# An unread 26-row product behind the second scores of the first attention, in the steps where the shared bank is free

## The reference

```
x = x + 0.5 * ffn0(layernorm(x))      # routed experts
x = x + attn0(layernorm(x))           # this case
x = x + 0.5 * ffn0(layernorm(x))
x = x + 0.5 * ffn1(...)
x = x + attn1(...)
x = x + 0.5 * ffn1(...)
```

```
qkv  = x @ qkv_w + qkv_b
attn = softmax(einsum('bnhd,bmhd->bhnm', q, k) * 8 ** -0.5)
out  = einsum('bhnm,bmhd->bnhd', attn, v) @ proj_w + proj_b
```

## Time and profile before

| what | us |
|---|---|
| median of 3 runs | 3365.65 |
| lowest, highest of them | 3340.04, 3366.84 |
| the profiled execution | 3353.67 |
| its span, first to last instruction | 3351.9 |
| first attention within the span | about 455 to 1335 |

### The profile page before, as it was taken

The page is one execution under the profiler, slowest core; times in us unless marked ns, Lnnn a source line. Parts: engine busy times, 40 slices in busy tenths (PEclk is TensorE's granted clock), DMA queues, the critical chain, the costliest instruction groups (busy, mean ns, idle before and its releaser), DMA issues. The chain is left out here.

```text
span 3351.9 us, 46625 instructions
## 1 busy us (share of the span) xinstructions
PE 2934.7 (88%) x15938; PEld 1757.2 (52%) x15938; DVE 2516.6 (75%) x6115; ACT 1773.0 (53%) x2711; POOL 928.1 (28%) x885
## 2 busy tenths in 40 slices
PE   6999959999999998899995689899799999989853
PEld 4666623443443443666663556566566666656432
DVE  6888767888888880788876797867366778797765
ACT  3444406777777775444435556454345555555544
POOL 2221121121111100212101355556323323343333
PEclk9999957999999996899995689989899999999965
DMA  4343432122122110343430000000000000000000
GB/s 127 77 100 80 95 102 93 57 93 84 66 93 84 66 49 6 111 93 79 101 77 1 1 7 20 19 19 19 32 13 13 13 7 14 13 7 26 7 7 25
DMA packets 71588, 167.20 MB, mean 50 GB/s; under 512 B 8792, under 2 KB 9400, under 8 KB 67128
## 3 DMA queue, kind: packets, MB, share of 16 engines
q1 hardware_dynamic: 69176, 160.03, 16.5%
q10 hardware_dynamic: 2176, 4.19, 0.3%
HBM read 120.67 MB, written 43.52 MB: 49 GB/s over the span
## 5 line engine op out<-in xcount | busy, mean ns | idle before, releaser
L706 DVE TENSOR_REDUCE att_mx<-att_pair 128x2 f32<-128x1024 f32 x512 | 617.0, 1220 | 132.5 <-PE att_pair L955 132.1
L881 ACT ACTIVATE att_pt<-att_pair 128x1024 f32<-128x1024 f32 x512 | 522.8, 1025 | 235.7 <-PE att_pair L965 233.1
L977 PE MATMUL att_o<-att_pt,att_vx 128*32 128x256 f32 x4096 | 335.5, 413 | 9.8 <-ACT att_oT L887 5.1
L955 PE MATMUL att_pair<-att_k,att_q 24*128 24x512 f32 x1024 | 272.4, 535 | 48.8 <-DMA att_k<-att_spread_k 14.2
L965 PE MATMUL att_pair<-att_q,att_k 26*128 26x512 f32 x1024 | 265.5, 520 | 0.0
L965 PEld LDWEIGHTS att_pair<-att_q,att_k 26*128 26x128 f32 x1024 | 98.5, 191 | 195.0 <-issue 168.1
L457 ACT ACTIVATE ffnA_h<-ffnA_up,b 128x512 f32<-128x512 f32 x144 | 98.7, 686 | 178.9 <-PE ffnA_up L105 177.2
L457 ACT ACTIVATE ffnB_h<-ffnB_up,b 128x512 f32<-128x512 f32 x144 | 98.6, 685 | 178.1 <-PE ffnB_up L105 176.4
L955 PEld LDWEIGHTS att_pair<-att_k,att_q 24*128 24x128 f32 x1024 | 100.3, 195 | 136.2 <-ACT att_pt L881 89.2
L977 PEld LDWEIGHTS att_o<-att_pt,att_vx 128*32 128x32 f32 x4096 | 91.6, 111 | 143.0 <-issue 123.4
L1897 ACT ACTIVATE att1k_sq<-att1k_k 128x512 f32<-128x512 f32 x128 | 76.2, 595 | 165.0 <-PE att1k_k L105 164.9
(11 more groups left out here) (538 smaller groups left out, 7787.8 us busy)
## 6 DMA issues: line engine op xcount, KB each, us to landing
ffnA_weights<-ffnA_weights SPq DMA_DIRECT2D x128, 256.0 KB, 5.6
att_q<-att_spread_q SPq DMA_DIRECT2D x16, 1024.0 KB, 4.9
att_k<-att_spread_k SPq DMA_DIRECT2D x16, 1024.0 KB, 4.8
att_spread_q<-att_qhi SPq DMA_DIRECT2D x32, 256.0 KB, 2.5
att_spread_k<-att_khi SPq DMA_DIRECT2D x32, 256.0 KB, 3.3
twk_hi<-ffnB_weights SPq DMA_DIRECT2D x32, 256.0 KB, 3.9
twk_lo<-ffnB_weights SPq DMA_DIRECT2D x32, 256.0 KB, 5.0
tgk_hi<-ffnB_weights SPq DMA_DIRECT2D x32, 256.0 KB, 6.0
```

Source lines behind the costliest of these rows:

```text
L706: v.tensor_reduce(top[b % 2][:, t, h:h + 2], pair("s", k)[:, :].rearrange("p (h n) -> p h n", h=2), AX, ALU.max, negate=True).then_inc(mx, 1)
L881: a.activation(pt[k % 8][:, :, :].rearrange("p h n -> p (h n)"), pair("t", k)[:, :], ACT.Exp, scale=scale).then_inc(p_, 1)
L955: last = pe.matmul(pair("s", k)[:, (j - j0) * 512:(j - j0 + 1) * 512], qb[b % 3][r, u, t * P:(t + 1) * P], kb[b % 3][r, u, :], start=True, ...
L977: last = pe.matmul(obank[j * BLOCK:(j + 1) * BLOCK, cols], vxb[b % 3][:, t, 4 * u + j, :], pt[(2 * g + j // 2) % 8][:, j % 2, cols], start ...
```

## The change

After the second scores of a step (`again`) TensorE now calls `keep_clock`. In steps in which no value in `misc` is still to be read it issues one more product of 26 rows by 512 columns, from the first head strip (partitions 0 to 25) of the same unit and tile, into `misc`. Nobody reads it, and it signals nothing. Before it stands `misc_free` of the next use of misc, so TensorE waits there for the reader of the last one. The step of each use is written beside it in `uses_of_misc`, and `misc_idle` holds the steps from two after a use up to the one before the next.

```diff
-        yield from (("x", 0), ("q", 0), ("k", 0), ("v", 0))
+        yield from ((-1, "x", 0), (-1, "q", 0), (-1, "k", 0), (-1, "v", 0))
...
-                yield "maxima", m - 1
+                yield STEPS * m + 2, "maxima", m - 1
...
-    misc_uses = list(uses_of_misc())
+    misc_order = list(uses_of_misc())
+    misc_uses = [(kind, k) for _, kind, k in misc_order]
     misc_number = {use: n for n, use in enumerate(misc_uses)}
+    misc_idle = {step: (kind, k) for (last, _, _), (next_, kind, k) in zip(misc_order, misc_order[1:]) for step in range(max(last, 0) + 2, next_)}
...
+        def keep_clock(k):
+
+            step = k + LAG
+            if step in misc_idle:
+                b, u, t, _ = place(k)
+                r = slice(0, SHIFTED)
+                misc_free(pe, *misc_idle[step])
+                pe.matmul(misc[:, :], kb[b % 3][r, u, t * P:(t + 1) * P], qb[b % 3][r, u, :], start=True, stop=True)
+
...
                 if 0 <= k < total:
                     again(k)
+                    keep_clock(k)
                 if STEPS * m + n + 1 < total:
                     scores(STEPS * m + n + 1)
```

More of the change, by code:

```diff
@@ L646, in uses_of_misc @@
             if now:
-                yield "maxima", m - 1
+                yield STEPS * m + 2, "maxima", m - 1
             if new:
-                yield "x", m + 1
+                yield STEPS * m + 5, "x", m + 1
             if old:
-                yield "out", UNITS * (m - 2) + 2
+                yield STEPS * m + 7, "out", UNITS * (m - 2) + 2
             if new:
-                yield "q", m + 1
-                yield "k", m + 1
+                yield STEPS * m + 9, "q", m + 1
+                yield STEPS * m + 13, "k", m + 1
             if old:
-                yield "out", UNITS * (m - 2) + 3
+                yield STEPS * m + 15, "out", UNITS * (m - 2) + 3
             if new:
-                yield "v", m + 1
+                yield STEPS * m + 17, "v", m + 1
             if old:
-                yield "final", m - 2
-                yield "proj", m - 2
+                yield STEPS * m + 21, "final", m - 2
+                yield STEPS * m + 23, "proj", m - 2
             if now:
-                yield "out", UNITS * (m - 1)
-                yield "out", UNITS * (m - 1) + 1
-    misc_uses = list(uses_of_misc())
+                yield STEPS * m + 25, "out", UNITS * (m - 1)
+                yield STEPS * m + 30, "out", UNITS * (m - 1) + 1
+    misc_order = list(uses_of_misc())
+    misc_uses = [(kind, k) for _, kind, k in misc_order]
     misc_number = {use: n for n, use in enumerate(misc_uses)}
+    misc_idle = {step: (kind, k) for (last, _, _), (next_, kind, k) in zip(misc_order, misc_order[1:]) for step in range(max(last, 0) + 2, next_)}
     def misc_free(pe, kind, k):
```

## The result

| | before | after |
|---|---|---|
| median of the runs, us | 3363.7 | 3416.1 |
| lowest, highest | 3340.0, 3366.8 | 3406.0, 3425.3 |
| ratio | | 1.0171, 95% interval 1.0115 to 1.0226 |
| the profiled execution, its span | 3353.7, 3351.9 | 3425.3, 3423.1 |
| mean granted clock | 0.908 | 0.893 |

The change costs 1.7%, by the ratio some 57 us (39 to 76); the two medians lie 52 us apart. Ratios compare fast runs alone: a run over 1.5% above the fastest of its kernel is left out. The forecast was 38 us, and the median lies inside its range. The span of the profiled execution is 71 us longer. The first attention alone became 79.6 us longer, and 8.5 of that came back in the keys stage of the second attention (615.1 to 606.6 us). That stage has none of the change, and over all 14 profiles it took between 606.6 and 619.3 us, at a mean clock between 0.81 and 0.83.

The account below looks back on a forecast made before the run. The prediction took a ring of second scores, exponential, first scores and weighing as the limit. 30.2 us for 13 full groups, 3 for m = 1 and 4.7 for the last groups made 38, on 3359.7: 3398 us, range 3372 to 3425.

Parts of the forecast that it names:

- The ring: First attention: second scores, exponential, first scores into that bank pair, weighing, next second scores; said to hold the pace.
- the three waits: Steps 11, 4 and 19 of each group: TensorE waits for misc's reader, costing 0.80, 0.48 and 0.71 us.
- the 0.10 of step 20: Step 20 of a full group: some 0.1 us of the added product's delay is left.
- step 4: Step 4 of a group: the product waits for the reader of the maxima, moving the weighing by 0.48 us.
- The seven other products: Steps 0, 1, 12, 20, 27, 28, 29: nothing except 0.10 us in step 20 and 0.23 in step 28.
- the walk: Step-by-step timing of the group from 703.09 in the first attention: the change adds 2.32 us per group.
- The clock: Granted clock in the first attention: no net change taken, nothing added to the forecast.
- The rival that the waits lower the clock: Clock falls at one of three thinner places in most groups; 13 groups add 30 us: 3428 us, chance 0.16.
- the balance: Products of steps 27 to 29 ahead of low-clock stretches set against places thinned by waits: clock effect nothing.
- the busy but slow stretch at the end: From 1258.8 to 1306.9, TensorE busy 44.8 of 48.1 us yet near the lower clock; added products should hardly raise it.
- The group m = 1: First attention, group m = 1: the same three waits and one more, mostly at the lower clock, 3 us.
- The late part: Last three groups of the first attention: 1.2 us in m = 15, 2.8 in m = 16, 0.7 in m = 17.

Follow-up runs that it names:

- The waits alone: The change with all its waits for the bank's reader but without the added product: 1.0088 of the kernel before, groups 51.50 us apart.
- the run with late steps: The change with its product only from the third step behind a use of misc on, five per full group: 1.0023 of the kernel before.
- the last run: The change with its wait in step 11 kept and only the product of step 11 left out: 1.0129 of the kernel before.
- the repeat: The change once more, unaltered, timed in another batch with a second profile: 1.0240 of the kernel before, median 3429.5 us.

## Why the prediction was right, and where its size was off

**The ring and the waits: right.** The largest term was the three waits, counted in full because no idle TensorE stands behind them. By the distances from the start of the first step named to the end of the last one:

| steps | before, us | after, us | more | forecast |
|---|---|---|---|---|
| 4 to 7 | 5.83 | 6.27 | 0.44 | 0.48 |
| 11 to 13 | 5.16 | 5.96 | 0.80 | 0.80 |
| 19 to 23 | 8.38 | 9.10 | 0.72 | 0.71 + 0.10 |
| 28 to 30 | 4.36 | 4.58 | 0.22 | 0.23 |

The sum is 2.17 against 2.32. Of the two small misses, the 0.10 of step 20 isn't there, and step 4 was 0.04 too dear. The waits alone gave 1.66, which leaves 0.51 for the products on top of them. The seven other products cost what the walk said, nothing but for step 28, and the run with late steps had 0.19 for five of them. That a product on the same strips adds 0.23 to the way held (0.21 in the last run). By the Trainium skill ("TensorE: Matmul & The Clock Gate", Part 3) a weight load overlaps running matmuls only when it goes to another group of rows, which would make it 0.43. The trace doesn't agree: after the change, the product's weights go into the first strip from 738.99, while the second scores from 738.88 still run on the first two strips, and the cost was 0.21.

**The clock: the term that was mis-sized.** The prediction put it at zero: "The new products of the steps 27 to 29 stand just ahead of such stretches, but the three waits make other places thinner. I set one against the other." In the middle groups it cost 42 us more than before, profile against profile. The prediction named a sign for this: "if the middle groups show a clock under 0.95 (clock falls)". They show 0.90 in this profile and 0.94 in the second, so by its own sign this part was wrong. The rival that the waits lower the clock had the sign, and 30 us for it, and the median of 3416 us lies between the forecast, 3398, and that rival, 3428. The direct costs in the middle groups were 28 us where 30.2 were forecast; the rest up to 57 is clock and the groups at both ends. That the total fell inside the range owes something to luck, because the range was drawn up to 3425 for this very rival, and the repeat at 1.0240 is above it.

The step that failed is the balance. The products did not keep the clock at step 30: three stretches still begin there. And at step 11, where none began before, six do. Falls at step 11 were seen only where the wait and the product of step 11 stand in one step, with other parts of the change around (without the product no fall there, without both none, and with step 11 alone none either). Which of the other parts it needs is open; step 12 is not it. It may instead be that the distance of the groups matters: all 26-row kernels with falls at step 11 have 52.0 us and no other has. Groups with a long stretch there come in rows (four, three and two) of about 58 us, as if each put the next in the same place. No run here varies the distance alone, so why the clock falls at step 11 stays open.

**That more of 26 rows wouldn't lift the clock: borne out.** The prediction argued it from the busy but slow stretch at the end. After the change m = 16 stands at 0.61, where it was 0.62 before, and the kernel with 26-row products at the end alone is at 0.67.

```profile
1258.80:1317.30 58.50, 53.48 (x358) 19.62 (x354) 2.89 (x9) 34.87 (x39) 0.00 (x0) 0.62 0.02 7
```

**The group m = 1** was put at 3 us, for "the same three waits and one more (step 15)". It doesn't have step 4, because its second scores begin in step 10. And the stage up to the start of m = 2 took 120.8 us in place of 122.8 in the profiles, so the 3 us can't be seen.

**The late part** was forecast at 4.7 us. m = 15 took 2.7 us less in the profiled execution (47.85 against 50.52), m = 16 took 3.6 more and m = 17 10.3 more:

```profile
1384.70:1414.90 30.20, 26.37 (x164) 10.92 (x160) 1.78 (x5) 11.98 (x14) 0.00 (x0) 0.56 0.00 1
```

Before, the same part took 19.9 us at 0.93. The eight products were put at 0.7 us in all, so most of this is clock too.

## What to carry to other kernels

An instruction that "waits only until a buffer is free" is not free itself: on an engine that executes in order, it holds up all behind it, and in a ring with no slack the whole wait is paid (1.66 us of the 2.17 a group here). Put filler where the trace shows the release already past, or behind the work that would be held up; here that cut the direct cost of a group from 2.17 to 0.68 us with the same 187 products, though the whole kernel was still 1.0% slower. Filler meant for the clock paid in neither form: on 26 rows it added time and the clock was no higher, and on all 128 rows the whole change cost as much (1.0176), with the time in longer groups in place of low clock. Before a difference in clock is put down to a change, profile the same kernel more than once: the same middle groups lost 7.5 us in one execution and 22 in two others.

## What the runs showed of the hardware that I had not expected

- With products on 128 rows the clock stood at 1.00 through 13 groups in a row, where the same products on 26 rows had 0.90, with the same busy share of 96%. The Trainium skill ("TensorE: Matmul & The Clock Gate", Part 1) has the clock set by how busy TensorE was of late; the share of time busy doesn't tell these two kernels apart. Rows and distance of the groups both differ between them.
- The clock fell though TensorE was never idle for long: at step 11 of the change the only idle stretch over 0.2 us in the 8 us ahead of each fall is the wait of 0.69 us.
- The kernel's own time moves by over 1% between executions (3323 to 3381 us in 31 runs of the kernel before), and the longer it is, the lower is its mean granted clock (0.917 at 3323 us, 0.897 at 3381), so that differences of under 0.5% are not settled by ten runs.
